# One loop of 128 expert jobs, with routing and the state-space scan laid into its slots

## The reference

```
expert FFN, for every token and each of 16 experts:
    scores = softmax over the 4 largest of (x @ router_w + router_b), 0 elsewhere
    gate, up = x @ gate_up_proj[e] + gate_up_bias[e]       # 128 each
    act = (clip(up, -7, 7) + 1) * min(gate, 7) * sigmoid(1.702 * min(gate, 7))
    out += scores[e] * (act @ down_proj[e] + down_bias[e])
state-space part, per channel d, with a = sigmoid(A_param):
    y[t] = sum over s <= t of C * a^(t-s) * B * x[s]  +  D * x[t]
    out = layer_norm(x + gelu(y) @ W_proj.T + b_proj)
```

## Time and profile before

| | |
|---|---|
| median of 3 runs | 902.07 us |
| the profiled execution, its own time | 903.93 us |
| its span | 902.2 us |
| PE, VectorE, ScalarE, GpSimd busy | 764.4, 533.8, 556.9, 232.9 us |
| mean granted clock of TensorE | 0.894 |

### The profile page before, as it was taken

How to read it: one execution, slowest core, us unless ns; L and a number is a source line. 1 busy time by engine, 2 the same in 40 slices (tenths; PEclk the granted TensorE clock), 3 DMA queues, 4 the chain that set the end, 5 groups by cost and what they waited for, 6 DMA issues and landing times.

```text
span 902.2 us, 11409 instructions
## 1 busy us (share of the span) xinstructions
PE 764.4 (85%) x3866; PEld 471.7 (52%) x3866; DVE 533.8 (59%) x1312; ACT 556.9 (62%) x801; POOL 232.9 (26%) x265
## 2 busy tenths in 40 slices
PE   4599999974568999999686769999998699999867
PEld 3477878753356877877453542322335423332355
DVE  5898888878557888888563552222236422322364
ACT  3555545445544545554423449999975599999643
POOL 6055555555423555555302000000000000000030
PEclk9999999995558999999676688999998799999967
DMA  9100000000000000000000000000000000000001
GB/s 284 45 1 1 1 1 0 1 1 1 0 1 1 0 1 1 1 0 1 1 0 0 1 0 1 2 1 1 1 2 1 0 1 1 1 1 1 3 1 47
DMA packets 10718, 9.22 MB, mean 10 GB/s; under 512 B 1584, under 2 KB 10240, under 8 KB 10368
## 3 DMA queue, kind: packets, MB, share of 16 engines
q1 hardware_dynamic: 9360, 7.01, 2.7%
q0 software_dynamic: 368, 1.38, 0.5%
q10 hardware_dynamic: 928, 0.06, 0.1%
HBM read 7.40 MB, written 1.05 MB: 9 GB/s over the span
## 4 chain that ended last, share of the span: by engine, by line
ACT 26%; issue 23%; POOL 21%; PE 18%; DVE 11%; POOLq 0%; ACTq 0%; DVEq 0%
ACT raw_w L597 22%; POOL act_lo L418 18%; PE bank L1374 2%; ACT xt L471 2%; PE bank L1124 2%; PE bank L1326 2%; PE bank L1327 2%; PE bank L1160 1%; PE bank L1126 1%; PE bank L1125 1%; DVE stats L692 1%; POOL rstd L397 1%; PE bank L1359 1%; DVE xn_lo L703 1%; PE bank L1173 1%
## 5 line engine op out<-in xcount | busy, mean ns | idle before, releaser
L597 ACT ACTIVATE raw_w<-bank,minus_c 128x1024 f32<-128x1024 f32 x256 | 259.7, 1161 | 7.9 <-DVE bank L1005 4.5
L418 POOL TENSOR_TENSOR act_lo<-act,act_hi 128x512 fp32r<-128x512 f32 x128 | 165.8, 1295 | 174.6 <-ACT act_hi L522 174.6
L515 ACT ACTIVATE glu<-bank,b_gate 128x512 f32<-128x512 f32 x128 | 88.1, 688 | 144.8 <-PE bank L1126 144.8
L1005 DVE TENSOR_TENSOR bank<-bank,fix 128x256 f32<-128x256 f32 x128 | 55.2, 433 | 191.5 <-PE bank L1359 191.5
L1374 PE MATMUL bank<-raw_w 128*9 128x512 f32 x1024 | 140.1, 610 | 0.0
L817 DVE TENSOR_SCALAR up<-bank,b_up 128x512 f32<-128x512 f32 x128 | 96.1, 751 | 35.8 <-PE bank L1126 35.8
L1124 PE MATMUL bank<-xn_hi,w_hi 128*128 128x512 f32 x256 | 102.2, 399 | 0.0
L1126 PE MATMUL bank<-xn_lo,w_hi 128*128 128x512 f32 x256 | 102.0, 399 | 0.0
L1125 PE MATMUL bank<-xn_hi,w_lo 128*128 128x512 f32 x256 | 101.1, 395 | 0.0
L827 DVE SCALAR_TENSOR_TENSOR act<-up,bank 128x512 f32<-128x512 f32 x128 | 87.9, 687 | 4.5
L821 DVE SCALAR_TENSOR_TENSOR bank<-glu,bank 128x512 f32<-128x512 f32 x128 | 87.6, 684 | 0.0
(11 more groups left out here) (188 smaller groups left out, 1218.6 us busy)
## 6 DMA issues: line engine op xcount, KB each, us to landing
raw_w<-in_gate_up SPq DMA_DIRECT2D x4, 512.0 KB, 9.9
x_tok<-in_x SPq DMA_DIRECT2D x4, 256.0 KB, 4.3
raw_w<-in_down SPq DMA_DIRECT2D x4, 256.0 KB, 9.9
sel_h<-in_sel_h POOLq DMA_DIRECT2D x1, 1024.0 KB, 9.4
grow<-in_grow SPq DMA_DIRECT2D x1, 1024.0 KB, 7.1
out<-x_tok SPq DMA_DIRECT2D x4, 256.0 KB, 2.3
raw_s<-in_squares SPq DMA_DIRECT2D x1, 512.0 KB, 7.2
sel<-in_sel POOLq DMA_DIRECT2D x1, 256.0 KB, 6.9
```

Of the source, the lines that this page charges most:

```text
L418: pool.tensor_tensor(act_lo[:, j % NACT, :], act[:, j % NACT, :], act_hi[:, j % NACT, :].bitcast(F32), ALU.subtract)\
L515: eng.activation(glu[:, j % 2, :], bank[:, G[j % 2], :], ACT.Gelu_apprx_sigmoid, bias=b_gate[:, e:e + 1]).then_inc(s["glu_ready"], 1)
L597: eng.activation(probs[:, u % NP, :], pair, ACT.Exp, bias=minus_c[:, b:b + 1])\
L1005: eng.tensor_tensor(pair, pair, turned, ALU.mult)\
```

## The change

The two blocks of 64 jobs become one loop of 128 slots (`JOBS`), with slots from -13 on for what must come first. Each engine's loop does in a slot its part of job `slot` and then what `side` gives it: every step of the chains `in` (take in, norm and routing of a chunk) and `ssm` (the whole chain from the addition of the first FFN to the routing of the second) whose base plus step equals the slot, and some single operations. The bases are 13 and 10 slots ahead of the loop for chunks 0 and 1, slots 2 and 9 for chunks 2 and 3, and for the scan chains slots 18, 34, 50 and 66, one slot behind the addition that they need. On GpSimd the side work stands before the low part of the job.

Further parts: G, U and O have one bank each instead of two (S keeps two); the three other banks serve the side work (`SIDE_T1`, `SIDE_T2`, `SIDE`), each with one place, and `side_free` makes PE wait until the use before was read. The y and z operations of the scan and the addition `ssm_out` go from VectorE to GpSimd, with the factor D applied by an additional ScalarE activation (`xn_direct`) and the factor B*C folded in the scan's input. The copy of the input goes from VectorE to ScalarE, the low parts of weight groups 2 and 3 and of the square matrices from VectorE to GpSimd, two memsets of 128x2048 from GpSimd to VectorE. The load of `sel_h` (1 MB) moves from the start to slot 80, as its place holds the Gelu's parts until then. `UP_ON_ACT` is 0, so every job's up half has its bias on VectorE and the branches of `up_on_act` are not taken. From `ffn1a` on only names of banks and counters change.

```diff
-HEADS = {"ffn0a": {7: 2}, "ssm": {16: 2}}
+JOBS = 2 * NC * E0
+UP_ON_ACT = 0
+BASE = {"in": (-13, -10, 2, 9), "ssm": tuple(E0 * (c + 1) + 2 for c in range(NC))}
+STEPS = {
+    "pe": {"in": {"take_in": 0, "t2": 4, "logits": 6, "scores": 10},
+           "ssm": {"t1": 0, "t2": 4, "proj": 10, "inner_t1": 11, "inner_t2": 15, "b_t1": 20, "b_t2": 24, "logits": 27,
+                   "scores": 34}},
+    "act": {"in": {"take_in": 0, "rows": 3, "hi": 5, "exp": 8, "out": 11},
+            "ssm": {"rows": 3, "copy": 5, "gelu": 8, "inner_rows": 14, "scale": 16, "b_rows": 23, "hi": 25, "exp": 31,
+                    "out": 35}},
+    "dve": {"in": {"stats": 0, "lo": 5, "pick": 6, "share": 9},
+            "ssm": {"stats": 0, "scan_in": 5, "scan": 6, "resid": 10, "inner_stats": 11, "b_stats": 20, "lo": 25,
+                    "pick": 28, "share": 32}},
+    "pool": {"in": {"norm": 1},
+             "ssm": {"norm": 1, "y": 7, "gelu_lo": 9, "inner_norm": 12, "add": 16, "b_norm": 21}},
+}
+SINGLE = {
+    "pe": {},
+    "act": {"split_small": -9, "split0": -6, "split1": -3, "split2": 0, "split3": 3, "split_squares": 11},
+    "dve": {"split_small": -9, "split0": -6, "split1": -2, "powers": 8},
+    "pool": {"split2_0": 1, "split2_1": 2, "split2_2": 4, "split3_0": 5, "split3_1": 6, "split3_2": 8,
+             "split_squares0": 12, "split_squares1": 13, "load_sel_h": 80},
+}
...
-        G, U, S, O = (0, 1), (2, 3), (4, 5), (6, 7)
+        G, U, S, O = 0, 1, (2, 3), 4
+        SIDE_T1, SIDE_T2, SIDE = 5, 6, 7
...
+        def side(engine, slot, chains, single={}):
+            for name, at in SINGLE[engine].items():
+                if at == slot:
+                    single[name]()
+            for chain in ("in", "ssm"):
+                for c in range(NC):
+                    for name, step in STEPS[engine][chain].items():
+                        if BASE[chain][c] + step == slot:
+                            chains[chain][name](c)
...
         @block.gpsimd
+            def ssm_y_z(c):
...
+                pool.wait_ge(s["scan_ready"], c + 1)
+                pool.tensor_tensor(ssm_y[:, b, :], ssm_sum[:, b * CH:(b + 1) * CH], back, ALU.mult)\
+                    .then_inc(s["ssm_step"], 1)
...
+                pool.tensor_tensor(ssm_z[:, b, :], xn_direct[:, b, :], ssm_y[:, b, :], ALU.add)\
+                    .then_inc(s["y_ready"], 1)
...
+            for slot in range(FIRST_SLOT, JOBS):
+                side("pool", slot, chains, single)
+                if slot >= 0:
+                    expert_lo(slot)
...
         @block.scalar
+            for slot in range(FIRST_SLOT, JOBS + 1):
+                if 0 <= slot < JOBS:
+                    expert_glu(slot)
+                if slot >= 1:
+                    expert_hi(slot - 1)
+                side("act", slot, chains, single)
...
         @block.vector
+            eng.memset(sel0_all[:].bitcast(F32), 0.0)
+            eng.memset(score_all[:].bitcast(F32), 0.0).then_inc(s["pads_ready"], 1)
...
+            for slot in range(FIRST_SLOT, JOBS + 2):
+                if 0 <= slot < JOBS:
+                    expert(slot)
+                if slot > E0 and slot % E0 == 1:
+                    add_out(slot // E0 - 1)
+                side("dve", slot, chains, single)
...
         @block.tensor
+            def side_free(name, i):
+                at = side_uses.index((name, i))
+                if at >= 1:
+                    before, nth_before = side_uses[at - 1]
+                    pe.wait_ge(s[side_read[before]], nth_before + 1)
+            def expert_in(j):
...
+                if j >= 1:
+                    pe.wait_ge(s["glu_ready"], j)
+                split_matmul(bank[:, G, :], w0_hi[:, e, 0, :], w0_lo[:, e, 0, :],
+                             xn_hi[:, at], xn_lo[:, at], True, True).then_inc(s["g_ready"], 1)
+                if j >= 1:
+                    pe.wait_ge(s["up_ready"], j)
+                split_matmul(bank[:, U, :], w0_hi[:, e, 1, :], w0_lo[:, e, 1, :],
+                             xn_hi[:, at], xn_lo[:, at], True, True).then_inc(s["u_ready"], 1)
+                if j >= 2:
+                    pe.wait_ge(s["act_ready"], j - 1)
...
+            def expert_down(j):
...
+                out = bank[:, O, :]
+                if e == 0:
+                    if j >= E0:
+                        pe.wait_ge(s["x_ready"], j // E0)
...
+            for slot in range(FIRST_SLOT, JOBS + 2):
+                if slot == 0:
+                    pe.wait_ge(s["cast_loaded"], 48)
+                    pe.wait_ge(s["pads_ready"], 1)
+                if 0 <= slot < JOBS:
+                    expert_in(slot)
+                if slot >= 2:
+                    expert_down(slot - 2)
+                side("pe", slot, chains)
```

More of the change, by code:

```diff
@@ L51 @@
 WQ, WK, WV, WO = 4, 5, 6, 7
-STAGES = {
-    "ffn0a": {"norm": 0, "take_in": 0, "stats": 0, "rows": 1, "t2": 1, "hi": 2, "lo": 2, "logits": 2, "pick": 3,
-              "exp": 3, "share": 4, "scores": 4, "out": 5, "split": 5},
-    "ssm": {"t1": 1, "stats": 1, "norm": 1, "rows": 2, "t2": 2, "copy": 3, "scan": 3, "gelu": 4, "gelu_lo": 4,
-            "proj": 5, "resid": 5, "inner_t1": 5, "inner_stats": 5, "inner_norm": 5, "inner_rows": 6,
-            "inner_t2": 6, "scale": 7, "add": 7, "b_t1": 9, "b_stats": 9, "b_norm": 9, "b_rows": 10, "b_t2": 10,
-            "hi": 11, "lo": 11, "logits": 11, "pick": 12, "exp": 12, "share": 13, "scores": 13, "out": 14},
+JOBS = 2 * NC * E0
@@ L69 @@
 }
-ONCE = {"ffn0a": {"split_small": 2, "powers": 3, "split_squares": 7}, "ffn1a": {"first": 11, "second": 12}}
+ONCE = {"ffn1a": {"first": 11, "second": 12}}
 ORDERS = {
-    "ffn0a": {
-        "pe": ["scores", "take_in", "t2", "logits"],
-        "act": ["split", "out", "hi", "rows", "exp"],
-        "dve": ["share", "split", "pick", "lo", "stats"],
-        "pool": ["norm"],
-    },
-    "ssm": {
-        "pe": ["b_t1", "scores", "logits", "proj", "inner_t1", "inner_t2", "t1", "b_t2", "t2"],
-        "act": ["out", "scale", "copy", "gelu", "rows", "b_rows", "inner_rows", "hi", "exp"],
-        "dve": ["share", "pick", "lo", "stats", "b_stats", "scan", "resid", "add", "inner_stats"],
-        "pool": ["b_norm", "gelu_lo", "inner_norm", "norm"],
-    },
     "ffn1a": {
```

457 lines of the change are left out of this document (232 added, 225 removed).

## The result

| | before | after |
|---|---|---|
| median of the runs | 901.76 us (4 runs, 901.18 to 902.25) | 876.2 us (4 runs, 874.2 to 879.77) |
| the profiled execution, its own time | 903.93 us | 875.9 us |
| its span | 902.2 us | 874.1 us |
| last addition of the experts at | 430.81 us | 407.01 us |
| mean granted clock of TensorE | 0.894 | 0.919 |

The ratio is 0.9721, with a 95% interval of 0.9689 to 0.9753. The kernel became 25.6 us faster where 42 were forecast: the direction, the range and the start of the loop hold, the gain is 61% of the forecast one. The loop should have lasted from 25.5 to 389.0, 363.5 us; it lasted from 26.29 to 407.01, 380.7.

The account below looks back on a forecast made before the run. PE was taken to bound the loop: start 25.5 + PE's own work 323.9 + stalls 33.6 + cold start and end 6.0 = 389.0 us, 41.8 less than before, so 860 us. Forecast 845 to 878 (70%), range 838 to 888.

Parts of the forecast that it names:

- Start of slot 0: Start of the expert loop: VectorE free for job 0 at 25.5 us (bounds 24 and 30), 15.5 us gained.
- PE's own work at the high level: PE in the loop: 128 jobs of 2.31 us, bias matmuls 5.3, side work 4.7 and 18.2; sum 323.9 us.
- All stalls 33.6: PE's waits in the loop: 24.6 us in four scan chunks, 7.0 in slots 0 to 17, 2.0 for O and scores.
- The table of lateness: Slot-by-slot sum of each engine's lateness; what exceeds PE's allowance (0.65 to 0.9 us) is a stall, 6.4 a chunk.
- Rival C: PE falls to the low clock in the loop's gaps; gain gone from 18 such jobs, 918 us with 25; 3%.
- a stretch of the loop below clock 0.9: One of the signs in the loop that would make the forecast wrong; a granted clock near 1.0 was expected.
- does not bind over the loop, only in slots: VectorE's total in the loop, 253 us of jobs plus 57 of side work, 310, stays under PE's 324.
- Rival D: Each of the loop's 20 table changes costs another 1.28 us: 25.6 more, 886 us; 6%.
- slot 10, Gelu waits for z: Slot 10 of the 16-slot pattern: Gelu waits for z, then 1.25 us and the table back; 1.6 us stall.
- O's single bank and the scores: PE waits for the addition at 7 passes, and scores of chunks 2 and 3 follow their share closely: 2.0 us.
- A: Rival: loop bound by PE, side work overlaps and stalls stay near 10 us, 23.6 less: 836 us; 17%.
- B: Rival: single banks turn the loop's 180 us of side work into PE time; decides at 75, half gives 916; 4%.

Follow-up runs that it names:

- the smoothed order with y and z on VectorE: Kernel after with share and last chunk's routing one slot later, powers' scan ahead of the loop, scan's y and z back on VectorE: 859.3 us, ratio 0.9524.
- the two loops at 1.00: Loops of the smoothed order with y and z on VectorE (859.3 us) and of the kernel after without changes of function table (852.5 us).
- three slots behind: Down matmuls three slots behind instead of two, on the smoothed order with y and z on VectorE plus two banks for U: 856.7 us, ratio 0.9513.
- the spread: Share and last chunk's routing one slot later, powers' scan ahead of the loop, against the kernel after: 860.9 us; with y and z on VectorE too, 859.3.
- the run with two more edges smoothed: Powers' scan ahead of the loop and last chunk's routing one slot later, on the kernel after with its share moved one slot: 860.9 us, ratio 0.9535.

## Why the prediction was right in direction and short in size

**Start of slot 0: right.** 25.5 was forecast and 26.29 measured for VectorE, within the bounds; the first matmul even stood at 22.94, at the low level, as the working had it possible. The pads' memsets ended at 5.13 and held the first statistics by some 0.5 us (5.05, before 4.52), ahead of an idle time of 4.60: they cost nothing.

**PE's own work at the high level: as forecast, as far as can be read.** Slots without side work take 2.31. The two bias matmuls cost 0.85 to 0.87 (0.66 forecast): from S at 174.93 to the second down matmul at 176.26 are 1.33 us, where 0.46 pass without them; that is 1.6 us in 8 passes. No run shows the 323.9 as a whole. The 360.85 us of the smoothed order with y and z on VectorE hold own work, stalls and end together; that they lie near the 363.5 is a weak sign.

**What PE waits for, and at what clock: here the gain was lost.** The forecast had "All stalls 33.6"; with its own 323.9 and 6.0 the measured 380.7 leave 50.8. The 17.2 between them are not mostly waiting: PE was idle 31.6 us (380.72 - 349.11), near the 33.6. The larger part is the term that the forecast put at nothing, "at a granted clock near 1.0". The loop at 0.96 of the clock means some 31 us at the low level (0.04 x 380.7 / 0.5), in which matmuls start 0.43 instead of 0.23 apart; about half of them, 15 us (an estimate), is PE's own work taking longer. 31.6 + 15 + 1.6 for the bias matmuls are 48 of the 50.8; waits shorter than 0.17 us, which a matmul's 0.40 covers, don't show as idle time. PE is busy 349.1 us here, and 337.3 and 335.4 in the two loops at 1.00. So the total of the waits was right in size; that the forecast had it right is in part luck, since its single terms were not:
- The waits were fewer and longer. Ten waits of 1.4 to 3.3 us make 21.6 of the 31.6; the working's largest terms were 2.8 and 1.6. In front of G six took 8.0 us, up to 1.8, where some ten of 1 to 1.6 were expected.
- "share 1.29", taken from the earlier trace rows, where no 128x512 operation of GpSimd ran. In slot 50 it took 3.25. The earlier trace rows had shown the same thing for the scan, 1.22 and 1.92, and I used it there and nowhere else. The table of lateness then had slot 2 of the pattern at 0.6; measured, slots 50 to 52 lost 5.4 more than with the share one slot on. Moving it made the loop 14.0 us shorter (12.3 between the medians), of the 17.2 by which it was too long: 6.2 of idle time and 7.8 of PE's busy time.
- The granted clock. Rival C had 18 jobs at the low level as the point where the gain is gone and was given 3%; it came true in small, with 31 us, some seven jobs' worth. The prediction's own sign, "a stretch of the loop below clock 0.9", came true too, over short stretches: from 183.65 to 189.4 PE ran at the low level throughout. The low stretches follow single waits, in a loop where PE is busy 92% of the time. The Trainium skill's rule that I leaned on (TensorE: Matmul & The Clock Gate, Part 1), that activity releases the low level, was applied to the mean of the loop; the rows show the level falling behind single waits.
- Slots where two side operations meet: the powers and a pick in slot 8, forecast at 2.8, share and statistics in slot 18, not in the table at all. Taking both apart made 3 us.

**VectorE "does not bind over the loop, only in slots": right in the sum, and too mild.** 322.8 of 380.7 us are busy; the forecast had 310 against PE's 324. Its spare is 0.33 us a slot, so a lateness of 3 us lasts nine slots if no side work comes between (an estimate, 3 / 0.33); the allowance that I had for one slot (0.65 to 0.9) says how late it may be, not how fast it recovers. The runs with two banks for U showed it.

**Table changes: price and stalls right, what follows them left out.** 1.28 a load and `exp` at once behind it, here too (173.49, 174.78). I took 12.4 us of them for stalls; taking 20 away shortened the loop by 25.1, of which 11.4 are idle time of PE and 13.7 its busy time at the higher clock. Rival D in its letter (twice as dear) fell; its 886 is nearer to the measured 876.2 than the forecast's 860, but for a reason that the rows don't have. What the Trainium skill's page (ScalarE: Activation LUTs, "What ACT_TABLE_LOAD costs") would add with its drain fell too: no run here shows one.

**y and z on GpSimd at 0.8 a chunk, and "slot 10, Gelu waits for z": no such wait is there;** the Gelu starts behind its table load at 206.00, z ended at 205.72. Still the kernel with both on VectorE is 4.5 us faster, by the clock and not by less idle time.

**O's single bank and the scores: right in size.** PE waited for the addition 3 times, 0.8 us in all, and twice, 1.9 us, for a share in front of the scores' transposes; 2.0 was forecast for both.

**The rest: nothing changes behind the loop, right;** the 4.3 us less there are within what fourteen executions show of themselves.

**The rivals.** A (836) would have needed stalls near 10; the best loop here with its table changes has some 28 (358.04 - 323.9 - 6.0, three slots behind). B's point, 75 us of stalls, was not reached: 50.8. The range was meant to reach from A's centre to D's, 836 to 886, and stands as 838 to 888; the measured time is inside by either.

## What to carry to other kernels

When side work is poured into a loop, cost each small operation next to what the other engines do in that same slot, not by its row in a quiet stretch; then look for the slot where two of them meet, for a wait of 2 to 3 us there can be paid twice, the second time by the clock. When a loop is longer than forecast, read PE's idle time and its busy time apart: the same instructions with more busy time are the clock, and a look at the waits alone doesn't find it. Spread came before buffers here: moving one step by one slot gave 12.3 us, a second PSUM bank for U gave 7 without the spread and nothing with it. And an engine with 1.98 us of work in a slot of 2.31 needs some nine slots to forget 3 us.

## What the runs showed of the hardware

- The share's VectorE operations with two inputs in SBUF end 0.08 to 0.09 us behind the 128x512 operation of GpSimd that was running when they began: 0.60, 0.75 and 1.30 us for 0.22. Those with one input (reduction 0.22, reciprocal 0.18) and those with one of two in PSUM (`glu * score` 685 ns, `act` 687 ns as a mean over the loop) keep their time. It goes the other way too: `act_lo` beside the scan that had begun before it took 1.93, and 2.90 beside the powers' scan of 2.29, instead of 1.30, and ends 1.05 to 1.08 us behind the scan each time. The Trainium skill states this (SBUF — State Buffer, "Who interferes with whom"): a VectorE instruction with two SBUF inputs contends with a GpSimd instruction that reads SBUF, over a pair of ports that is an exclusive lock. For the 128x512 operations the rows agree, in both directions. Beside GpSimd's power on 128x4 (L437, 181.35 to 182.39 in the run with the moved share) two such operations of the share kept their 0.22, so not every GpSimd operation costs this. The forecast's share had this rule against it and did not weigh it.
- In the kernel after the low level of the clock came with the end of a wait of 3.28 us, for some 6 us of work, and four matmuls behind one of 1.81 (209.34 to 210.46), for 3 us. But the length of a wait doesn't decide it. In the run with two more edges smoothed two equal waits ended differently:

```profile
200.23 0.50 PE L1202 MATMUL bank<-xn_hi,w_hi 128*128 128x512 f32 x1 [1.81 <-ACT glu L600]
...
201.42 0.63 PE L1203 MATMUL bank<-xn_hi,w_lo 128*128 128x512 f32 x1
...
249.78 0.50 PE L1202 MATMUL bank<-xn_hi,w_hi 128*128 128x512 f32 x1 [1.81 <-ACT glu L600]
...
251.04 0.39 PE L1204 MATMUL bank<-xn_lo,w_hi 128*128 128x512 f32 x1
```

  A matmul of 0.63 us is at the low level, one of 0.39 at the high one. In the loop without table changes waits of 2.82 and 2.73 us left the level high. The four waits of 1.38 to 1.40 us of the run with y and z on VectorE left it high too.
- Behind the loop the same 2334 PE instructions took 466.0 to 471.4 us in fourteen executions, with mean clocks of 0.87 and 0.88: a difference of 4 us between two spans can lie in a part that no edit touches.
